# Cross attention of a decoder kernel: the DMA moves of each group of squares sent in two parts, by tiles

## The reference, cut to what matters

```
kv_rope = kv_c * cos + rotate_half(kv_c) * sin             # (16, 1500, 64)
scores  = einsum('bhsr,bhlr->bhsl', q_r, k_r)              # (16, 16, 56, 1500)
attn    = softmax(scores, axis=-1)
ctx_c   = einsum('bhsl,bld->bhsd', attn, kv_rope)          # (16, 16, 56, 64)
```

## Time and profile before

| | us |
|---|---|
| median of 3 runs | 3181.08 |
| lowest and highest run | 3168.54, 3193.82 |
| profiled execution, first to last instruction | 3214.1 |
| of that, first to last move of the three stages (by SP's rows) | 409.7, 412.1 and 408.6 |

### The profile page before, as it was taken

One profiled execution on the slowest core, in us unless ns is written; L12 is line 12 of the kernel. 1 busy time (PEld: TensorE's weight loads), 2 busy tenths in 40 slices (PEclk: granted clock), 3 DMA queues, 4 the chain that ended last, 5 costly groups with the idle time before them and its releaser, 6 DMA issues. The chain is left out here.

```text
span 3214.1 us, 48214 instructions
## 1 busy us (share of the span) xinstructions
PE 2927.4 (91%) x17993; PEld 1703.9 (53%) x17997; DVE 1876.2 (58%) x3657; ACT 1245.7 (39%) x1997; POOL 873.8 (27%) x743
## 2 busy tenths in 40 slices
PE   4899999869999899899999989989899999677999
PEld 3755555545455463455556557753455555346444
DVE  6568888642222357778875143347788885654222
ACT  3456666511111242555554122222456554424221
POOL 4325555400343124333333000004333333211000
PEclk8899999979999899999999999999999999888999
DMA  1148898614122112377775010012367775001111
GB/s 32 53 124 179 177 181 172 135 29 134 35 105 92 52 43 78 88 152 171 168 148 138 11 42 25 26 43 78 77 154 165 153 167 134 15 12 24 39 40 33
DMA packets 221444, 299.25 MB, mean 93 GB/s; under 512 B 127178, under 2 KB 149052, under 8 KB 218764
## 3 DMA queue, kind: packets, MB, share of 16 engines
q1 hardware_dynamic: 220348, 294.39, 39.2%
q10 hardware_dynamic: 864, 1.77, 0.2%
HBM read 120.52 MB, written 21.38 MB: 44 GB/s over the span
## 5 line engine op out<-in xcount | busy, mean ns | idle before, releaser
L1796 ACT ACTIVATE l2x_shared<-l2x_shared,l2x_a_low 128x1500 f32<-128x1500 f32 x112 | 173.3, 1547 | 160.4 <-DVE l2x_shared L1748 156.5
L1796 ACT ACTIVATE l1x_shared<-l1x_shared,l1x_a_low 128x1500 f32<-128x1500 f32 x112 | 173.3, 1548 | 159.6 <-DVE l1x_shared L1748 156.1
L1796 ACT ACTIVATE l0x_shared<-l0x_shared,l0x_a_low 128x1500 f32<-128x1500 f32 x112 | 173.3, 1548 | 146.4 <-DVE l0x_shared L1748 145.7
L1660 PE MATMUL l0x_a_S_ps<-l0x_kt,l0x_a_q 64*128 64x366 f32 (+1 forms) x896 | 176.0, 507 | 3.5 <-DVE l0x_shared L1748 3.0
L1660 PE MATMUL l1x_a_S_ps<-l1x_kt,l1x_a_q 64*128 64x366 f32 (+1 forms) x896 | 178.6, 515 | 0.6 <-DVE l1x_shared L1748 0.6
L1660 PE MATMUL l2x_a_S_ps<-l2x_kt,l2x_a_q 64*128 64x366 f32 (+1 forms) x896 | 178.4, 515 | 0.6 <-DVE l2x_shared L1748 0.6
L2040 DVE TENSOR_TENSOR l0f_times_up<-l0f_gate,l0f_U 128x448 f32<-128x448 f32 x64 | 39.8, 621 | 236.9 <-PE l0f_U L1958 236.9
L2009 ACT ACTIVATE l0f_gate<-l0f_G 128x448 f32<-128x448 f32 x72 | 39.2, 545 | 310.7 <-PE l0f_G L1953 310.7
L1353 POOL TENSOR_TENSOR l2x_q_straight<-l2x_q_straight,l2x_q_crossed 128x448 f32<-128x448 f32 x48 | 54.5, 1136 | 339.6 <-DVE l2x_q_crossed L1344 339.6
L1695 PE MATMUL l1x_a_C_ps<-l1x_space,l1x_v 128*64 128x192 f32 (+1 forms) x1024 | 121.8, 373 | 21.7 <-DMA l1x_space<-l1x_a_blocks 18.9
L1695 PE MATMUL l2x_a_C_ps<-l2x_space,l2x_v 128*64 128x192 f32 (+1 forms) x1024 | 117.8, 363 | 20.8 <-DMA l2x_space<-l2x_a_blocks 17.2
(11 more groups left out here) (678 smaller groups left out, 6478.7 us busy)
## 6 DMA issues: line engine op xcount, KB each, us to landing
l0x_space<-normed SPq DMA_DIRECT2D x192, 128.0 KB
l1x_space<-normed SPq DMA_DIRECT2D x192, 128.0 KB
l2x_space<-normed SPq DMA_DIRECT2D x192, 128.0 KB
l0x_space<-l0x_a_blocks SPq DMA_DIRECT2D x186, 96.0 KB, 3.3
l1x_space<-l1x_a_blocks SPq DMA_DIRECT2D x186, 96.0 KB, 3.3
l2x_space<-l2x_a_blocks SPq DMA_DIRECT2D x186, 96.0 KB, 3.4
l0f_gu<-in_L_ffn_gu SPq DMA_DIRECT2D x36, 256.0 KB, 2.6
l0x_a_q<-l0x_qa SPq DMA_DIRECT2D x32, 224.0 KB
```

The source lines that it names most:

```text
L1660: last = pe.matmul(S_ps[:, 2 * pair + rows_, 0:w], q[lane, b % 2, k * 128:(k + 1) * 128], kt[lane, b % 2, pair * W1:pair * W1 + w], start= ...
L1796: act.activation(p[:, n % 2], p[:, n % 2], ACT.Exp, bias=low[:, n % 2, 1:2], scale=-1.0, accum_out=den[:, b % 2, k:k + 1]).then_inc(exp_re ...
```

## The change

`move` waits for `valued` first, and then sends its group in two parts. Part one (tiles 0 and 1 of the group) goes as soon as these two tiles are in squares; part two (the remaining two tiles for g = 0, the remaining one for g = 1) goes when the last tile of the group is. Each part is again twelve DMAs over 32 partitions, with runs of 2048 bytes (part one of both groups, part two of g = 0) or 1024 bytes (part two of g = 1). A batch has 48 moves where it had 24, with the same bytes. The counts that PE and DVE wait for double from 192 to 384.

```diff
+    PARTS = (((0, 2), (2, 4)), ((0, 2), (2, 3)))
+    MOVED = 16 * 12 * 2
...
         def move(eng, b, g, lanes):
 
-            eng.wait_ge(inner_blocked, T * b + FIRST[g] + COUNT[g])
-            eng.wait_ge(outer_blocked, T * b + FIRST[g] + COUNT[g])
             if b > 0:
                 eng.wait_ge(valued, 2 * (b - 1) + g + 1)
-            for l in lanes:
-                for qi in range(4):
-                    if qi != l:
-                        eng.dma_start(*part_at(g, l, qi)).then_inc(moved[g][b % 2], 16)
+            for first, end in PARTS[g]:
+                eng.wait_ge(inner_blocked, T * b + FIRST[g] + end)
+                eng.wait_ge(outer_blocked, T * b + FIRST[g] + end)
+                for l in lanes:
+                    for qi in range(4):
+                        if qi != l:
+                            to, source = part_at(g, l, qi)
+                            eng.dma_start(to[:, first * JB:end * JB], source[:, first * JB:end * JB]).then_inc(moved[g][b % 2], 16)
...
-                            pe.wait_ge(moved[g][b % 2], 192 * (b // 2 + 1))
+                            pe.wait_ge(moved[g][b % 2], MOVED * (b // 2 + 1))
...
-                        dve.wait_ge(moved[g][(b - 1) % 2], 192 * ((b - 1) // 2 + 1))
+                        dve.wait_ge(moved[g][(b - 1) % 2], MOVED * ((b - 1) // 2 + 1))
```

## The result

The changed kernel takes 3724.68 us (median, 3721.37 to 3728.6), against 3181.41 for the kernel before: a ratio of 1.169, 95% interval 1.1649 to 1.1731 (the two medians alone give 1.171). It is 543 us slower. The profiled execution spans 3726.1 us.

The account below looks back on a forecast made before the run. SP's issue queue was to become the bound: its work of 1735.9 us against stages of 1230.4 gives 505.5, 484 after the earlier start, plus 16 of waits, so +500: 3181 to 3681 us, range 3560 to 3800.

Parts of the forecast that it names:

- The issue price: On SP's queue, a half move was taken to cost 0.635 us to issue, like a whole one.
- The bound from below: On SP, all moves at 0.55 us an issue instead of 0.635: 193 us less, 3488 us.
- rivals 1 and 3: On SP, cheaper issues: first 0.37 us, about 3153, chance 0.04; third 0.48 us, about 3345, chance 0.08 including up to 3560.
- SP as the new bound: 24 more issues a batch make SP's cycle 35.99 us against 24.77 for PE, 11.2 us a batch more.
- PE's two waits: PE waits for moves before its value matmuls: about 1.6 us for g = 0 and 9.6 for g = 1.
- some 500 us: PE's idle time before its value matmuls (L1699) was to grow from 56.5 us to this, mostly for `blocks`.
- rival 2: PE's clock halves after waits; if not covered, 45 x 5 = 225 us on top, 3906 us; chance 0.08.
- The cover that I named: PE's 3.5 to 5 us lost at half speed eat its g = 0 wait, then SP's 6 us slack before `valued`.
- The sum: Over the three stages: 505.5 us more, 484 after the earlier start, plus 16 of SP's waits: +500, median 3681.
- the 33 us between them: The median of the runs was put 33 us below the profiled execution: 3714 became 3681.
- SP's work: SP's three stages: 1015.8 us with small gaps, plus 1134 added issues at 0.635 us, 720.1: 1735.9 us.
- the early start: At batch 0 of each stage part one leaves two tiles earlier: 7.1 us gained, 3 x 7.1 in all.

Follow-up runs that it names:

- the fastest kernel here: The kernel before, its moves unsplit, with 8 of the 24 a batch issued by ACT, two at a time: 3156.83 us, 0.9918 of before.

## Why the prediction was right, point by point

- *The issue price.* 0.635 us taken, 0.634 measured (591 ns and the same gap). The bound from below, 0.55, and rivals 1 and 3 are gone, as the run with 64-byte parts shows too.
- *SP as the new bound.* Shown by its timeline, with 1.6 us of pauses in 1777, and by the run that moved 12 issues to ACT and won 300 us. The cycle was put at 35.99 us; the batch shown has 36.89.
- *PE's two waits.* Put at 1.6 us before the first group and 9.6 before the second. In the timeline of PE they are, in two cycles:

```profile
1617.81 0.91 PE L1699 MATMUL l1x_a_C_ps<-l1x_space,l1x_v 128*64 128x192 f32 x4 [5.81 <-DMA l1x_space<-l1x_a_blocks]
1637.15 2.83 PE L1699 MATMUL l1x_a_C_ps<-l1x_space,l1x_v 128*64 128x256 f32 x12 [3.54 <-DMA l1x_space<-normed]
1657.50 0.91 PE L1699 MATMUL l1x_a_C_ps<-l1x_space,l1x_v 128*64 128x192 f32 x4 [7.22 <-DMA l1x_space<-l1x_a_blocks]
1674.94 1.52 PE L1699 MATMUL l1x_a_C_ps<-l1x_space,l1x_v 128*64 128x256 f32 x12 [1.00 <-DMA l1x_space<-normed]
1694.42 0.91 PE L1699 MATMUL l1x_a_C_ps<-l1x_space,l1x_v 128*64 128x192 f32 x4 [7.14 <-DMA l1x_space<-l1x_a_blocks]
```

  From 1657.50 to 1694.42 the cycle is 36.9 us, near the 36.0 of the prediction, and its waits are 1.0 and 7.1. The cycle before, with a long issue in it, takes 39.7 us, with 3.5 and 7.2. The pattern is right. What the prediction didn't put into these two waits is PE's own half speed: PE is busy for 28.5 us of the 36.9, where a batch took 24.77, and these 4 us come out of the wait for `blocks`. For the same reason "some 500 us" of idle time were 429.
- *PE's clock (rival 2).* It falls behind the waits, to 0.50 in the window shown above, and the time doesn't notice, since SP hardly ever waits for PE. The cover that I named was there.
- *The sum.* The time came out 43.7 us above 3681, in the range. The mechanism was right, and the 43.7 us are what is left of three errors, one of which has the other sign. The largest is the step from the profiled execution to the median: I took the 33 us between them over to the new kernel. But the changed kernel's profiled execution is only 1.4 us from its median. The unsplit variant with the new order of waits spans 3173.9 us with 34.1 us of waits before its value matmuls, where the execution that I worked from spans 3214.1 with 56.5. My execution was a slow one of its kernel: its three stages, from first score to last value matmul, take 36.5 us more than in that variant, with 22.4 us more of these waits, and a full queue swallows them. This term is 31.6 us. The second is SP's work: its rows add up to 1753.7 us in the three stages, where 997.8 + 720.1 = 1717.9 were expected. Of the 35.8 us, 18.6 are moves (long issues) and 17.2 are SP's other issues. The gaps of its timeline add up to 23.8 us, where 18 of small gaps and 16 of waits were taken, so the stages are 25.5 us longer than the sum had them. The third goes the other way: outside the stages the program took 1948.7 us, 35.0 less than before, where the early start was to bring 21.3. Most of the other 13.7 are a term that the sum doesn't have: from the end of SP's last issue in a stage to the last value matmul it is 3.8 to 5.4 us now, and 7.7 to 9.3 before, 12.7 in the three stages. That this missing term makes the forecast look better is luck.
- *The intent of the change.* I had 56.5 us as the most that earlier parts could bring. The prediction names the early start as lost behind a full queue. It doesn't say that earlier parts could bring hardly any of it in this form even with room on the queue: after the last tile of a group twelve issues still follow, as before, so the last landing comes no sooner than by the shorter transfer (2.0 us instead of 3.4). And part one of the second group stands behind the fetch that waits for tile 6's scores, so in SP's order it can't leave two tiles early: over all 48 batches of the changed kernel it starts 1.8 us or more after the last squares.

## What to carry to other kernels

Before a DMA is split, read the issuing queue's timeline: count x issue price, plus everything else on the queue, against the pace of the loop. Here the price was 0.59 us plus a gap of 0.04 whatever the bytes, and the queue was 84% full. Look also at what stands ahead of the new part in that queue's order, since it can leave no earlier than that. By this sum a split can help a landing only if fewer issues follow the last piece of data than before; no run here has such a split. If the same number follows, share the issues among queues, as the fastest kernel here does. And when a change makes another engine the bound, sum that engine's work to an absolute time; don't add a difference to an execution that holds waits the new bound will swallow.

## What the runs showed of the hardware

An issue of a move over 32 partitions took 507 ns at least on SP and 591 to 592 at the median, for 64 to 4096 bytes per partition (592 to 596 in the run with whole moves on both queues). On ACT the median was 525 to 614 ns. ACT issues DMAs while one of its activations runs: two issues from 1506.95 to 1508.14 beside an exponential from 1506.22 to 1507.76. So 8 issues a batch on ACT cost the exponentials nearly nothing; I had placed them in its pauses because I expected the opposite.
